# Cross attention: the first scores of a batch in eight steps of two heads, the chain of their maxima one step later

## The chip, the cores and the metric
The kernel runs on one core of a Trainium2 chip. Times are microseconds on the device for one execution, from three runs; the profile is of one further execution. TensorE does matmuls, VectorE and ScalarE read its results from PSUM banks, GpSimd does elementwise work in SBUF, and DMA queues (issued by SyncE, and here also by ScalarE) move data.

## The reference, cut to what matters
Two transformer layers over 8 batches of 112 tokens with 256 features and 16 heads of 16. The part that matters is multi-head attention, which stands three times: cross attention of 112 queries to 375 keys (first layer), self attention (second layer), cross attention to the same 375 tokens with other weights (second layer), then an MLP.

```python
def mha(q, k, v):
    scores = jnp.einsum('bqhd,bkhd->bhqk', q, k) / jnp.sqrt(d)
    attn = jax.nn.softmax(scores, axis=-1)
    out = jnp.einsum('bhqk,bkhd->bqhd', attn, v)
    return out.reshape(B, Nq, C)
x = x + mha(...) @ cross_o_w + cross_o_b
```

The softmax subtracts the largest score of each query and head. The kernel therefore makes the scores twice: once with queries on the partitions, for the maxima ("first scores"), and once transposed, keys on the partitions, with the negative maximum added inside the matmul ("transposed scores"), which go through the exponential and straight into the product with the values.

## The kernel before, in words
`attend` builds both cross attentions and the self attention. Work goes in slots, one per batch. In slot b the engines finish batch b, make the first scores and maxima of batch b+1 (`LAG` is 1 in cross attention), do the output projection of batch b-1 (the tail), and prepare keys, values and normalised context of later batches (the fills). Slot -1 is a preparing slot: it has first scores and fills, but no transposed scores and no tail. Slots -1 to 6 have first scores; slot 6 has no key fills, slot 7 has no first scores any more.

A cross attention slot has steps u = 0 to 12. Each engine has its own list of instructions in a fixed order, written out by `pe_slot`, `act_slot`, `dve_slot` and `pool_slot`, and the engines meet at semaphores. What TensorE does in a step, in this order:
- four transposed scores of unit u (L651 to L661), two banks in turn, each waiting for the exponential two units back;
- a tail part in steps 1, 3 and 5 (`TAIL_AT`, L679);
- a fill (`FILL_AT`, L607): K0 in step 1, K1 in 3 (keys), V0 in 7, V1 in 9 (values), T0 in 10, T1 in 12 (transposition of the context);
- the first scores of heads `S_AT[u]` to `S_AT[u+1]` (`pe_scores`, L627): one matmul of 375 columns per head, into three banks in turn, so that a head waits until VectorE has reduced the head three before it (`max_done`, L636);
- in step `MAX_AT` the transposition of the maxima (`pe_max_t`, L644), which waits for VectorE's chain (`nm_step`, L645);
- four matmuls with the values (L663 to L677) for the unit of the step before.

VectorE in the same step order: tail work, then for each head of the step a maximum over its 375 scores (L798). After the last head, in step `MAX_AT`, comes the chain of the maxima: four small steps that split the maxima into three bf16 parts (L803, L805, L807, L809), the wait for TensorE's transposition, and the copy of its result (L812); behind that the normalisation of a later context (L766, L769). ScalarE in step `LOAD_MAX_AT` issues the DMA that writes the three parts beside the queries (`load_max`, L848); the first transposed scores of the next slot wait for it (L654). GpSimd splits the keys further (L831, L833) and adds the bias to the new values (L839) after ScalarE has copied a V fill out of PSUM.

Before the change the heads stood 3, 3, 2, 3, 3, 2 in steps 0 to 5, and the chain in step 7:

```python
S_AT = [0, 3, 6, 8, 11, 14, 16, 16, ...] if cross else [0, 2, 4, 4, 4, 4]
LOAD_MAX_AT = 8
MAX_AT = 7 if cross else 3
```

Of the kernel before, what the change touches and what calls it, by code (L numbers as in the profile page):

```python
# [535 lines left out]
def attend(nc, sh, ctx, sems, name, cross, ln, wkv, bk, bv_row, wo, bo_row, gate, stacks, first, ahead=None):  # L536
# [12 lines left out]
    LAG = 1 if cross else 2  # L549


    S_AT = [0, 3, 6, 8, 11, 14, 16, 16, 16, 16, 16, 16, 16, 16] if cross else [0, 2, 4, 4, 4, 4]
    K0, K1, V0, V1, T0, T1 = range(6)
    FILL_AT = {1: K0, 3: K1, 7: V0, 9: V1, 10: T0, 12: T1} if cross else {}
    MID_AT = {4: 0, 6: 1}
    LOAD_MAX_AT = 8
    MAX_AT = 7 if cross else 3
    TAIL_AT = {1: 0, 3: 1, 5: 2} if cross else {1: 0, 2: 1, 4: 2}

    def sb(n, shape, dt=F32):  # L560
# [66 lines left out]
    def pe_scores(pe, b, par, lo, hi, cnt):  # L627
        for i in range(lo, hi):
            if i == 0 and isinstance(b, int) and b == 0:

                pe.wait_ge(stacks.more["stacked"][0], stacks.more["stacked_count"])
            if cross and i == 0:
                pe.wait_ge(stacked[par][0], cnt * 16 * NTERM)
            if cross and i * HS == HC:
                pe.wait_ge(stacked[par][1], cnt * 16 * NTERM)
            wait(pe, max_done, NS * b + (i - 2 if i else 0))  # L636
            for h in range(i * HS, (i + 1) * HS):
                o = (h - i * HS) * T
                w = L if cross else T
                keys_h = sh.k_st[par][0:DEEP, h, 0:w] if cross else sh.k_all[0:DEEP, h, bass.ds(b * T, T)]  # L640
                last = pe.matmul(score[i % 3][:, o:o + w], sh.q_all[0:DEEP, h, bass.ds(b * T, P)], keys_h, start=True, stop=True)  # L641
            last.then_inc(s_psum, 1)

    def pe_max_t(pe, b):  # L644
        pe.wait_ge(nm_step, 4 * b + 4)  # L645

        wait(pe, nm_done, b)
        pe.transpose(nm_bank, nparts[:, :, :].rearrange("t a h -> t (a h)"),
                     sh.ident_bf[0:T, 0:T]).then_inc(nm_psum, 1)
# [49 lines left out]
    def pe_slot(pe, b, par, cnt, has_e, has_s, has_tail):  # L699
        for u in range(NU + 1):  # L700
# [6 lines left out]
            if has_s:  # L707
                pe_scores(pe, b + LAG, (par + LAG) % 2, S_AT[u], S_AT[u + 1], cnt[1])
                if u == MAX_AT:
                    pe_max_t(pe, b + LAG)  # L710
# [3 lines left out]
    def act_slot(act, b, par, cnt, has_e, has_s, has_tail):  # L714
        for u in range(NU + 1):
            if has_e and u < NU:
# [3 lines left out]
                act.activation(prob[u % 2][0:rows, :], score_t[u % 2][0:rows, 0:GH * T], ACT.Exp).then_inc(exp_done, 1)  # L720
            if has_s and cross and u == LOAD_MAX_AT:
                load_max(act, b + LAG, (par + LAG) % 2)
# [36 lines left out]
    def dve_norm_context(dve, b):  # L759

        if not isinstance(b, int) or b > 0:
            dve.wait_ge(fill_psum, fill_no(b - 4, T1) + 1)
        for t in range(NT):
            x_in = sh.ctx[:, bass.ds(b, 1), t, :]
            if ln:
                dve.tensor_scalar(xn[:, t, :], x_in, sh.ctx_mean[:, bass.ds(b, 1), t], sh.ctx_rstd[:, bass.ds(b, 1), t],  # L766
                                  ALU.subtract, ALU.mult).then_inc(xn_done, 1)
            else:
                dve.tensor_copy(xn[:, t, :], x_in).then_inc(xn_done, 1)  # L769

    def dve_slot(dve, b, par, cnt, has_s, has_tail, norm_next):
        for u in range(NU + 1):
# [18 lines left out]
            if has_s:  # L791
                n = b + LAG
                for i in range(S_AT[u], S_AT[u + 1]):
                    dve.wait_ge(s_psum, NS * n + i + 1)
                    if i == 0:
# [3 lines left out]
                                      AX_X, ALU.max, negate=True).then_inc(max_done, 1)  # L799
            if has_s and u == MAX_AT:  # L800
                dve.wait_ge(max_done, NS * (n + 1))
# [10 lines left out]
                dve.tensor_copy(nm_t[(par + LAG) % 2][:, :], nm_bank[0:3 * H, :]).then_inc(nm_done, 1)  # L812
            if norm_next and u == MAX_AT:
                dve_norm_context(dve, b + 3)
# [33 lines left out]
    def load_max(eng, b, par):  # L848

        eng.wait_ge(nm_done, b + 1)  # L850
        eng.dma_start(sh.q_all[DEEP:AUG, :, bass.ds(b * T, T)], nm_t[par][:, :]).then_inc(nm_in[par], 16)
# [280 lines left out]
def first_layer(nc, sh, ins):  # L1132

    with ExitStack() as ctx:
# [6 lines left out]
                     tensor_first=[(sh.wq_in, 16 * 8)], mod_first=[(sh.mod_done, NM)], bank_first=[(sh.mod_done, NM)])  # L1141
        w_all = 16 * 13
        at = attend(nc, sh, ctx, sems, "a0", True, True, sh.wkv0, sh.bcol[:, 1, :], 0, sh.wo0, 1, None, pj, {
            "tensor": pj.more["banks_read"] + md.more["banks_read"] + [(sh.consts_done, 4)],
            "gpsimd": pj.more["x_read"], "sync": []}, {
# [54 lines left out]
def self_attention(nc, sh):  # L1200

    with ExitStack() as ctx:
# [4 lines left out]
                     {n: stack for n in ("full", "rest", "part")})  # L1207
        pad_set = sems.new("pad_set")
        at = attend(nc, sh, ctx, sems, "a1", False, False, None, None, 2, sh.wo1, 3, 0, pj, {
            "tensor": pj.more["banks_read"], "gpsimd": pj.more["x_read"] + [(gate_in, 32)],  # L1210
            "sync": pj.more["banks_read"] + [(pad_set, 3)]})
# [39 lines left out]
def cross_attention(nc, sh, ins):  # L1251

    with ExitStack() as ctx:
        sems = ctx.enter_context(Semaphores(nc))
        mlp_in = sems.new("mlp_in")
        pj = project(nc, sh, ctx, sems, "p2", 1e-6, lambda c, b: sh.bcol[:, 4, c:c + 1], lambda c, b: sh.bcol[:, 5, c:c + 1],
                     sh.wq2, sh.bcol[:, 6, :], False, {"xn": Room(sh.v_space), "xt": Room(sh.gate_space[0])})
        at = attend(nc, sh, ctx, sems, "a2", True, False, sh.wkv2, sh.bcol[:, 7, :], 4, sh.wo2, 5, None, pj, {
            "tensor": pj.more["banks_read"], "gpsimd": pj.more["x_read"], "sync": []}, {"tensor": [], "scalar": [], "vector": []})
        block = ctx.enter_context(nc.Block())  # L1260
# [73 lines left out]
```

## Time and profile before

| | |
|---|---|
| time, median of 3 runs | 636.75 us (636.18 to 638.23) |
| profiled execution | 636.35 us, span 634.6 us |
| granted TensorE clock, mean | 0.865 of full speed |
| PE busy | 489.4 us (77% of the span) |
| DVE busy | 336.0 us (53%) |
| ACT busy | 251.8 us (40%) |
| POOL busy | 167.2 us (26%) |
| key transfers (93.8 KB each) | 2.2 us from issue to landing, median |

PE is TensorE's matmuls, PEld its weight loads (one load per matmul, which can run under the matmul before), DVE VectorE, ACT ScalarE, POOL GpSimd, SP SyncE; a "q" behind a name is that engine's queue. A row of a timeline gives start, duration, engine, line and operation, then output and inputs, the count of merged instructions, and in brackets the idle time of the engine before it and what ended that time. A matmul's end is modelled, so that rows of PE can overlap by a little; from the start of one group to the start of the next is what is read here. The shares are means over parts with different limits: the cross attentions' slots run from about 72 to 230 us and from about 411 to 565 us, the self attention lies between them, loading before and the MLP after.

### The profile page before, as it was taken

To read this page: it belongs to the slowest core of one execution; us is meant where nothing else is said; L and a number is where in the kernel's file an instruction comes from. 1 tells how busy PE (TensorE), PEld (TensorE's weight loads), DVE (VectorE), ACT (ScalarE), POOL (GpSimd) and SP (SyncE) were. 2 spreads that over 40 slices of the span, in tenths; PEclk is the share of its full clock that TensorE was granted. 3 is DMA by queue.
4 is the path that set the end of the run, shared out by engine and by line. 5 is a ranking of instruction groups with operands and counts; after the bars stand their busy time and mean duration, and the time that the engine had idled before them with its cause. 6 is when DMAs were issued, how large, how long until landed. Compare 5 with 4: busy or idle time off the path is not lost. (4 is left out here: it accounts for less than half of the span.)

```text
span 634.6 us, 12540 instructions
## 1 busy us (share of the span) xinstructions
PE 489.4 (77%) x4242; PEld 306.0 (48%) x4242; DVE 336.0 (53%) x835; ACT 251.8 (40%) x523; POOL 167.2 (26%) x182
## 2 busy tenths in 40 slices
PE   3846579999999951942399756089999999968997
PEld 3542245555565530621266424045555555537896
DVE  6594255675565429763257364464755564423441
ACT  1202136656665530210134413036566666452221
POOL 7121033422233109810000028033332333100000
PEclk9956579999999975875579957599999999997999
DMA  8996722121222003187400032662221222000000
GB/s 187 226 307 159 132 74 67 48 74 44 67 75 70 7 29 89 43 187 205 104 19 26 9 133 73 175 152 54 69 62 50 73 73 56 21 2 1 15 23 22
DMA packets 66884, 52.38 MB, mean 83 GB/s; under 512 B 11327, under 2 KB 65039, under 8 KB 66839
## 3 DMA queue, kind: packets, MB, share of 16 engines
q1 hardware_dynamic: 66023, 51.61, 32.3%
q8 instruction: 27, 0.44, 0.3%
q10 hardware_dynamic: 816, 0.17, 0.1%
q14 instruction: 18, 0.15, 0.1%
HBM read 25.66 MB, written 6.44 MB: 51 GB/s over the span
## 5 line engine op out<-in xcount | busy, mean ns | idle before, releaser
L798 DVE TENSOR_REDUCE a_nmax<-bank 112x1 f32<-112x375 f32 (+1 forms) x288 | 140.3, 549 | 128.7 <-PE bank L641 128.4
L720 ACT ACTIVATE a_prob<-bank 128x448 f32<-128x448 f32 (+2 forms) x224 | 120.7, 544 | 114.3 <-PE bank L659 110.5
L641 PE MATMUL bank<-k_stack,q_stack_all 96*128 96x375 bf16 x256 | 69.5, 340 | 30.8 <-DMA q_stack_all<-q_parts 16.5
L675 PE MATMUL bank<-a_prob,v_tokens 128*17 128x112 f32 (+2 forms) x1792 | 88.1, 269 | 1.6 <-ACT a_prob L720 1.4
L659 PE MATMUL bank<-q_stack_all,k_stack 99*128 99x112 bf16 (+1 forms) x768 | 72.2, 216 | 0.7 <-issue 0.7
L659 PEld LDWEIGHTS bank<-q_stack_all,k_stack 99*128 99x128 bf16 x768 | 43.3, 98 | 35.0 <-issue 29.1
L612 PE MATMUL bank<-k_stack_all,wkv 128*128 128x375 f32 x128 | 55.3, 560 | 3.6 <-ACT a_kp L732 2.3
L641 PEld LDWEIGHTS bank<-k_stack,q_stack_all 96*128 96x128 bf16 (+1 forms) x256 | 24.9, 100 | 66.9 <-issue 43.4
L675 PEld LDWEIGHTS bank<-a_prob,v_tokens 128*17 128x17 f32 (+2 forms) x1792 | 29.9, 96 | 46.0 <-issue 30.1
L617 PE MATMUL bank<-wkv,k_stack_all 128*128 128x256 f32 (+1 forms) x192 | 48.4, 388 | 0.0
L839 POOL TENSOR_TENSOR v_tokens<-v_tokens,bias_rows 128x256 f32<-128x256 f32 (+1 forms) x48 | 33.2, 706 | 50.0 <-ACT v_tokens L743 50.0
L730 ACT ACTIVATE k_stack_all<-bank,bias_columns 128x375 f32<-128x375 f32 x32 | 18.4, 574 | 63.3 <-PE bank L612 63.3
L617 PEld LDWEIGHTS bank<-wkv,k_stack_all 128*128 128x128 f32 (+1 forms) x192 | 33.6, 188 | 3.6
L612 PEld LDWEIGHTS bank<-k_stack_all,wkv 128*128 128x128 f32 x128 | 25.6, 220 | 16.9 <-ACT a_kp L732 4.5
L624 PE MATMUL bank<-ident,a_xn 128*128 128x128 f32 (+1 forms) x96 | 19.7, 320 | 16.1 <-DVE a_xn L769 4.1
L831 POOL TENSOR_TENSOR k_stack_all<-k_stack_all,v_all 128x375 f32<-128x375 f32 x16 | 14.3, 896 | 65.3 <-ACT v_all L732 65.3
L1108 ACT ACTIVATE mlp_hid<-bank,bias_hidden 128x224 f32<-128x224 f32 x32 | 14.3, 448 | 38.5 <-PE bank L1057 38.5
L696 PE MATMUL bank<-wo,a_ot 128*112 128x256 f32 x96 | 28.1, 418 | 1.3 <-ACT a_ot L725 1.3
L1067 PE MATMUL bank<-k_stack_all,mlp_hid 128*112 128x256 f32 x128 | 28.3, 379 | 0.0
L1057 PE MATMUL bank<-mlp_xt,k_stack_all 128*128 128x224 f32 x128 | 27.0, 372 | 1.4 <-DVE mlp_xt L1027 1.4
L1057 PEld LDWEIGHTS bank<-mlp_xt,k_stack_all 128*128 128x128 f32 x128 | 25.8, 203 | 2.3 <-DVE mlp_xt L1027 1.7
L930 POOL MEMSET k_stack<- 99x144 bf16 x4 | 0.8, 234 | 96.4 <-POOLq L94 96.4
(138 smaller groups left out, 690.1 us busy)
## 6 DMA issues: line engine op xcount, KB each, us to landing
k_stack<-a_kp SPq DMA_DIRECT2D x96, 93.8 KB, 2.2
k_stack<-v_all SPq DMA_DIRECT2D x96, 93.8 KB, 2.2
q_stack_all<-q_parts SPq DMA_DIRECT2D x36, 224.0 KB, 4.4
q_parts<-p_q_part SPq DMA_DIRECT2D x4, 672.0 KB, 4.9
k_stack_all<-k_parts SPq DMA_DIRECT2D x12, 224.0 KB, 4.5
ctx_tokens<-in_ctx_dram SPq DMA_DIRECT2D x2, 1024.0 KB
k_stack_all<-in_L_xcond_mlp_w_dram SPq DMA_DIRECT2D x2, 1024.0 KB
gate<-gate_rows SPq DMA_DIRECT2D x2, 896.0 KB
```

Of the source, the lines that this page charges most:

```text
L612: last = pe.matmul(cx[:, 0:L], wkv[:, c, m * P:(m + 1) * P], ct[par][:, c, :], start=c == 0, stop=c == CH - 1)
L617: last = pe.matmul(cx[0:rows, (t % 2) * C:(t % 2 + 1) * C], ct[1 - par][:, c, t * P:t * P + rows], wkv[:, c, C:2 * C], start=c == 0, stop= ...
L624: last = pe.transpose(cx[:, t * P:t * P + rows], xn[0:rows, t, c * P:(c + 1) * P], sh.ident[0:rows, 0:rows])
L641: last = pe.matmul(score[i % 3][:, o:o + w], sh.q_all[0:DEEP, h, bass.ds(b * T, P)], keys_h, start=True, stop=True)
L659: last = pe.matmul(score_t[u % 2][:, j * T:(j + 1) * T], keys_h, sh.q_all[0:AUG, h, bass.ds(b * T, T)], start=True, stop=True)
L675: last = pe.matmul(pv[32 * j:32 * j + D + 1, g * T:(g + 1) * T], sh.v_sb[par][0:rows, t, h, :], prob[u % 2][0:rows, j * T:(j + 1) * T], st ...
L696: last = pe.matmul(tb[0:T, 0:C], ot[:, c, :], wo[:, c, :], start=c == 0, stop=c == CH - 1)
L720: act.activation(prob[u % 2][0:rows, :], score_t[u % 2][0:rows, 0:GH * T], ACT.Exp).then_inc(exp_done, 1)
L798: dve.tensor_reduce(nmax[:, i * HS:(i + 1) * HS], score[i % 3][0:T, 0:HS * w].rearrange("t (h k) -> t h k", k=w), AX_X, ALU.max, negate=Tr ...
L839: pool.tensor_tensor(v, v, sh.brow[0:keys[t], bv_row, :].rearrange("p (h d) -> p h d", d=D), ALU.add).then_inc(v_done, 1)
L1057: last = pe.matmul(sh.bank[1 + m % 4][:, 0:N2], w1[:, c, m * P:(m + 1) * P], xt[:, c, :], start=c == 0, stop=c == CH - 1)
L1067: last = pe.matmul(y_bank[j][0:T, 0:C], hid[:, m, j * T:(j + 1) * T], w2[:, m, :], start=m == 0, stop=m == NH - 1)
```

## The change
Three constants of `attend` change, for cross attention. The sixteen first scores of a batch stand two in each of steps 0 to 7, the chain of the maxima with TensorE's transposition stands in step 8, and the DMA issue on ScalarE in step 9. Self attention keeps its lists (`LOAD_MAX_AT` is used in cross attention alone). Matmuls, reduces, transfers and buffers stay the same in number and shape; what changes is where they stand in the lists of TensorE, VectorE and ScalarE.

```diff
-    S_AT = [0, 3, 6, 8, 11, 14, 16, 16, 16, 16, 16, 16, 16, 16] if cross else [0, 2, 4, 4, 4, 4]
+    S_AT = [0, 2, 4, 6, 8, 10, 12, 14, 16, 16, 16, 16, 16, 16] if cross else [0, 2, 4, 4, 4, 4]
     K0, K1, V0, V1, T0, T1 = range(6)
     FILL_AT = {1: K0, 3: K1, 7: V0, 9: V1, 10: T0, 12: T1} if cross else {}
     MID_AT = {4: 0, 6: 1}
-    LOAD_MAX_AT = 8
-    MAX_AT = 7 if cross else 3
+    LOAD_MAX_AT = 9
+    MAX_AT = 8 if cross else 3
```

## Rows read from the trace of the kernel before

**Rows 1.** Busy time by stretch, one slot: us, busy (count) per engine, clock, DMA, GB/s
```profile
108.08:127.25 19.17, 18.77 (x201) 10.90 (x197) 11.27 (x27) 11.90 (x26) 6.35 (x8) 1.00 0.25 62
```
**Rows 2.** Timeline of the same slot, TensorE's matmuls: start, duration, engine, line, operation
```profile
112.40 0.74 PE L641 MATMUL bank<-k_stack,q_stack_all 96*128 96x375 bf16 x2
...
113.07 0.39 PE L675 MATMUL bank<-a_prob,v_tokens 128*17 128x112 f32 x8
...
115.08 0.64 PE L641 MATMUL bank<-k_stack,q_stack_all 96*128 96x375 bf16 x3
...
116.18 1.19 PE L641 MATMUL bank<-k_stack,q_stack_all 96*128 96x375 bf16 x3
...
117.30 0.39 PE L675 MATMUL bank<-a_prob,v_tokens 128*17 128x112 f32 x8
...
118.74 0.48 PE L641 MATMUL bank<-k_stack,q_stack_all 96*128 96x375 bf16 x2
...
119.15 0.39 PE L675 MATMUL bank<-a_prob,v_tokens 128*17 128x112 f32 x8
...
119.47 0.37 PE L659 MATMUL bank<-q_stack_all,k_stack 99*128 x4
...
119.77 0.39 PE L675 MATMUL bank<-a_prob,v_tokens 119*17 119x112 f32 x8
...
120.30 1.95 PE L617 MATMUL bank<-wkv,k_stack_all 128*128 128x256 f32 x8
...
122.09 0.21 PE L648 MATMUL bank<-ident_bf,a_nparts 112*128 112x112 bf16 x1
...
122.23 0.39 PE L675 MATMUL bank<-a_prob,v_tokens 128*17 128x112 f32 x8
```
**Rows 3.** Timeline of the same slot, VectorE: reduces, output addition, first and last chain step
```profile
115.44 2.82 DVE L798 TENSOR_REDUCE a_nmax<-bank 112x1 f32<-112x375 f32 x6 [1.41 <-PE bank L641]
...
119.06 0.42 DVE L785 TENSOR_TENSOR x_tokens<-bank,x_tokens 112x256 f32 x1 [0.79 <-PE bank L696]
...
119.40 0.99 DVE L798 TENSOR_REDUCE a_nmax<-bank 112x1 f32<-112x375 f32 x2
...
120.43 0.17 DVE L803 CAST a_nparts<-a_nmax 112x16 bf16<-112x16 f32 x1
...
121.05 0.17 DVE L809 TENSOR_TENSOR a_nparts<-a_nrest,a_nparts 112x16 bf16<-112x16 f32 x1
```
**Rows 4.** Timeline of the preparing slot of the first layer, VectorE and TensorE
```profile
78.90 3.73 DVE L798 TENSOR_REDUCE a_nmax<-bank 112x1 f32<-112x375 f32 x8 [0.67 <-PE bank L641]
...
82.88 0.82 DVE L805 TENSOR_TENSOR a_nrest<-a_nmax,a_nparts 112x16 f32<-112x16 f32 x1
...
83.94 0.17 DVE L809 TENSOR_TENSOR a_nparts<-a_nrest,a_nparts 112x16 bf16<-112x16 f32 x1
...
84.16 0.10 PEld L648 LDWEIGHTS bank<-ident_bf,a_nparts 112*128 112x128 bf16 x1 [1.18 <-DVE a_nparts L809]
...
84.23 1.08 PE L617 MATMUL bank<-wkv,k_stack_all 128*119 128x256 f32 x4
```
**Rows 5.** Timelines of two slots, GpSimd's additions and a chain step beside one
```profile
123.02 1.44 POOL L839 TENSOR_TENSOR v_tokens<-v_tokens,bias_rows 128x256 f32<-128x256 f32 x2 [0.80 <-ACT v_tokens L743]
...
139.82 0.90 POOL L833 TENSOR_TENSOR a_kp<-k_stack_all,a_kp 128x375 bf16<-128x375 f32 x1 [1.75 <-ACT a_kp L736]
139.91 0.85 DVE L809 TENSOR_TENSOR a_nparts<-a_nrest,a_nparts 112x16 bf16<-112x16 f32 x1
```
**Rows 6.** Timeline of the first slot, the issue of the maxima's DMA
```profile
123.08 0.79 ACTq L851 DMA_DIRECT2D q_stack_all<-a_nm_t  x1
```
**Rows 7.** Waits of weight loads in slot 6, first layer, then second: us, times, longest
```profile
PEld bank L641 <- DVE a_nmax L798: 2.1, 7, 0.4
...
PEld bank L641 <- DMA k_stack<-v_all: 1.0, 1, 1.0
```
**Rows 8.** Waits of weight loads over six slots, 88 to 205 us: us, times, longest
```profile
PEld bank L624 <- ACT k_stack_all L750: 2.1, 6, 1.0
```

## The prediction, made before the changed kernel ran

> **What bounds the kernel now.** I read the page first, then the busy time by stretch, then the timeline of one slot engine by engine, and last who waited for whom. The change touches only the slots of the two cross attention layers, so everything is read from one such slot, the one from 108.08 to 127.25 us. There TensorE has work for 18.77 of 19.17 us at a granted clock of 1.00, which is the 2.4 GHz level; VectorE has 11.27, ScalarE 11.90, GpSimd 6.35 [rows 1]. TensorE carries out its list in order, so a slot lasts as long as its matmuls plus the stops inside that list. The matmuls stay the same; the forecast is the difference of the stops.
>
> I write S14 for the score matmul of head 14, h14 for its reduce on VectorE, and "values", "transposed scores" for the two groups of four in each step. A score of head i goes to bank i mod 3 and so waits until the reduce of head i-3 is done.
>
> **Stops that the change removes.** The two scores of step 2 begin at 112.40 and the values behind them at 113.07: 0.67 us. An undisturbed pair takes 0.41 (118.74 to 119.15), so 0.26 is a stop. The three of step 4 take 1.12 (116.18 to 117.30); undisturbed they would take 0.41 plus 0.16 for a third head (375 columns at the 2.4 GHz level), so 0.55 is a stop [rows 2]. VectorE shows the cause: six reduces without a gap from 115.44, 0.47 each, which TensorE has to follow [rows 3]. Together 0.81 us per slot. With two heads per step these stops go: S5, S7, S9 and S11 each need the reduce of three heads before, which lies at least one whole step back and, but for S9 and S13, has a fill or a tail behind it; for S9 I count the reduce done just in time.
>
> **A stop that stays in another place.** S13 needs h10. VectorE works on the output addition of the tail at 119.06 and takes the next reduce at 119.40 [rows 3]; in the new order that reduce is h10, done at 119.87. In step 4 of before the values start 0.45 after the end of the reduce that the last score waits for (115.44 + 3 x 0.47 = 116.85, values 117.30), so the values of step 6 start at 120.32. Without a stop they would start at 119.77 + 2 x 0.16 = 120.09 [rows 2]. Cost 0.23 (bounds 0 and 0.26, the stop of the pair above).
>
> **The stop that the change adds.** Today S14 and S15 stand in step 5 and the transposition of the maxima in step 7 behind the V0 fill; TensorE reaches it at 122.09, long after VectorE's chain of four small steps (120.43 to 121.05 + 0.17 = 121.22) [rows 2, 3]. In the new order S14 and S15 stand behind the V0 fill in step 7, and between them and the transposition in step 8 lie only one group of values and one of transposed scores. Call Y the start of the first matmul behind the V0 fill (122.09 in this slot).
> - TensorE's side: pair of scores 0.41, values 0.32 (119.15 to 119.47), transposed scores 0.30 (119.47 to 119.77), transposition 0.14 (122.09 to 122.23) [rows 2]. Without a wait the next work starts at Y + 1.17.
> - VectorE's side: a reduce starts 0.36 after its score (115.08 to 115.44), two reduces and the gap to the chain take 1.03 (119.40 to 120.43), the chain 0.79 [rows 2, 3]. The chain ends at Y + 2.18. In the slot that only prepares (below) TensorE does wait here today: chain ends at 83.94 + 0.17, weight load at 84.16 after 1.18 us of waiting, next matmul at 84.23 [rows 4]. So 0.12 more: Y + 2.30.
>
> The stop is 1.13 us if nothing disturbs the chain. Queued behind the waiting transposition are all of TensorE's work of steps 8 to 12 and the next slot; nothing of it can pass.
>
> **What disturbs the chain.** GpSimd adds the bias to the values of the V0 fill, two additions that start 0.93 after the point that I call Y and last 1.44 (123.02 to 124.46); today that is after the chain. In the new order the chain's second step comes at Y + 1.6 and lies inside them. In this trace a chain step that meets a GpSimd addition waits to its end: GpSimd 139.82 to 140.72, the chain's fourth step from 139.91 to 140.76 instead of 0.17 us [rows 5]; in the preparing slot the second step took 0.82 in the same way [rows 4]. By this the second step ends near Y + 2.3 to Y + 2.4 instead of Y + 1.77 and the chain 0.5 to 0.6 later; I take 0.55. Its bounds are 0 (the steps slip between the additions) and 0.68 (the longer of the two holds, 0.85 for 0.17). The stop is then 1.68.
>
> The Trainium skill, page "SBUF — State Buffer", section "SBUF: two separate sides", says that a VectorE operation with two SBUF inputs and a GpSimd operation that reads SBUF take a shared port pair as an exclusive lock, and that the later one blocks fully. The holds just told agree; no row of before shows these two bias additions against a chain step. By the rule the stop is 1.68, by a chain that runs free it is 1.13.
>
> **The rest of the step that moves.** The copy of the transposed maxima and the DMA that spreads them (one issue on ScalarE's queue) move with the transposition. The issue is at 123.08, 4.2 us ahead of the next slot [rows 1, 6]. From the transposition to the slot's end remain all steps but one (0.62), and the issue stands behind the exponential of step 9 instead of step 8: I count 3 us or more from issue to need, against 2.2 for the larger key transfers on the page's list. Cost 0; if that cover were gone, the excess would stop the first transposed scores. VectorE's context normalisation also follows the chain and must be done by the T0 fill of step 10, one step (0.62) fewer away than now, but clear of GpSimd's two additions: cost 0, bound 0.3. SP's queue has nothing that moves, and its key transfers gain time.
>
> **The sum.** Each layer has eight slots with first scores.
> - Slots 0 to 5: 1.68 + 0.23 - 0.81 = +1.10 each; 12 of them, +13.2 us.
> - Slot 6 has no key fills, so today its scores stop more often: 7 waits with 2.1 us in the first layer, of which some 0.16 each is the ordinary loading gap, so 1.0 real; about 0.9 goes (bounds 0 and 2.1). In the second layer it also waits 1.0 us for keys by DMA [rows 7]; the eighth score comes a step later and the slot before grows behind that issue, so 0.9 more goes. 1.68 - 0.9 and 1.68 - 1.8: +0.7 together.
> - The preparing slot (-1), where VectorE sets the pace: today eight reduces run without a gap from 78.90 while the V0 fill runs under the last ones [rows 4]. In the new order S14 waits for that fill: from the end of h10 it is 0.45 until the fill starts (as to the values in step 4), 1.79 for it (120.30 to 122.09) [rows 2], 0.36 and 0.95 for the two reduces, 3.55 against 5 x 0.47 = 2.35 now; and h10 ends some 0.4 later, since h6 and h7 come behind the K1 fill and not ahead of it (2 x 0.47, less one reduce by which that fill starts earlier). That is +1.6, less 0.65 of a hold that today's chain has there (82.88, 0.82 for 0.17), plus 0.55: +1.5 each, +3.0 (bounds 0.9 and 2.0 each).
>
> Together 13.2 + 0.7 + 3.0 = +16.9 us. The profiled execution took 636.35 us (634.6 of span), so 653.3. It lies 0.4 under the median of 636.75, less than the sum can tell; I say 653.
>
> **Rivals.**
> 1. The chain runs free of GpSimd: 12 x (1.13 + 0.23 - 0.81) + (2 x 1.13 - 2.7) + 2 x 0.95 = 8.1, so 644.4 us. For it: the hold depends on which engine starts first, and the casts of the chain were never seen held. Against: two additions without a gap cover 1.4 us, just where the chain's two-input steps fall.
> 2. Faster. The stop before the transposition is made up in steps 9 to 12, if these wait for ScalarE and not for TensorE: then only the removed stops count, 12 x 0.58 + 2.7 gained, 3.0 lost in the preparing slots, near 629.7. It decides from about 1.2 us recovered per slot. For it: ScalarE has over half of the slot in work [rows 1]. Against: over six slots TensorE's loads waited 2.1 us for ScalarE's copies of the context, six times, the largest such sum there, 0.35 per slot [rows 8], and what ScalarE works on in these steps is made by TensorE behind the stop, so it cannot run ahead.
> 3. The removed stops do not come back as time, because the exponentials or key copies of steps 2 to 5 take over the pace: +12 x 0.81 and +2.7 on top, 666 us. Against: each stop that I count follows a reduce [rows 3], and TensorE has hardly a gap beside them [rows 1].
>
> **Chances.** Forecast (held chain) 0.60, rival 1 0.22, rival 2 0.06, something between (most of the stop made up, within 0.3%) 0.05, rival 3 0.07. A measurement of this kernel tells 0.3% (1.9 us) from no change. Faster 0.06, same 0.05, slower 0.89. The range goes from 642 (rival 1 with S13 at nothing, 644.4 - 12 x 0.23) to 658 (the forecast with the longer hold in all 16 slots, and nothing saved in slot 6); about 2 in 10 lie outside.
>
> **What would show it.** In the new trace: TensorE's weight load of the maxima's transposition waiting 1 to 2 us for the chain's last step in every slot; scores in pairs with no stop but one in step 6; two-input chain steps of 0.5 to 0.8 us beside GpSimd's bias additions; slots 1 us longer at an unchanged clock. It is wrong if the transposition does not wait, or if the slots do not grow by what it waits less 0.6.

## The result, and the profile after

The changed kernel takes 665.9 us (median of four runs, 662.3 to 669.3) against 637.5 for the kernel before (636.2 to 642.9, four runs): ratio 1.043 with a 95% interval of 1.034 to 1.052. It is slower, as forecast, but by 28.4 us and not by 16.9, and it lies 8 us above the top of the range, 658. The profiled execution took 668.65 us.

The page of the changed kernel (busy us, share of the span, instructions by engine):

```profile
span 666.9 us, 12540 instructions
...
PE 497.2 (75%) x4242; PEld 311.3 (47%) x4242; DVE 336.6 (50%) x835; ACT 251.1 (38%) x523; POOL 166.2 (25%) x182
```

The span grew by 32.3 us with the same number of instructions. TensorE's busy time grew by 7.8 (489.4 before), although its list has the same matmuls: some ran slower. The rest, 24.5, is time in which it stood.

Busy time by stretch: the slot that answers to [rows 1], then every stretch inside the slots in which the granted clock stood at 0.50, the 1.2 GHz level:

```profile
111.70:132.30 20.60, 18.68 (x201) 10.87 (x198) 11.19 (x27) 11.87 (x26) 6.24 (x8) 1.00 0.23 58
...
170.80:174.20 3.40, 3.40 (x37) 1.59 (x35) 0.19 (x1) 1.97 (x4) 1.36 (x2) 0.50 0.01 3
...
191.30:194.60 3.30, 3.30 (x22) 2.08 (x21) 1.05 (x3) 1.03 (x3) 0.64 (x1) 0.50 0.02 6
...
440.40:447.20 6.80, 5.75 (x22) 3.47 (x21) 1.46 (x5) 2.33 (x5) 1.37 (x2) 0.50 0.31 82
...
481.50:484.80 3.30, 3.30 (x37) 1.84 (x30) 0.00 (x0) 1.93 (x4) 1.37 (x2) 0.50 0.01 3
...
501.90:505.30 3.40, 3.40 (x30) 1.69 (x28) 0.00 (x0) 1.62 (x4) 1.37 (x2) 0.50 0.03 8
...
563.40:566.60 3.20, 3.20 (x27) 1.78 (x25) 0.00 (x0) 1.00 (x3) 0.60 (x1) 0.50 0.02 3
```

The first line is the forecast slot: 1.43 us longer at the 2.4 GHz level, with TensorE's work the same to 0.1 us. The other six are what the forecast did not have; the long one, from 440.40, follows the preparing slot of the second layer. Behind the preparing slot of the first layer the clock is low for 6.8 us in both kernels; elsewhere in its slots the kernel before has no such stretch.

The timeline of that slot, TensorE and its weight loads, VectorE, GpSimd and the DMA issue (answers to [rows 2, 3, 5, 6]):

```profile
121.22 0.42 DVE L785 TENSOR_TENSOR x_tokens<-bank,x_tokens 112x256 f32 x1 [0.80 <-PE bank L696]
121.56 1.90 DVE L798 TENSOR_REDUCE a_nmax<-bank 112x1 f32<-112x375 f32 x4
...
121.84 0.73 PE L641 MATMUL bank<-k_stack,q_stack_all 96*128 96x375 bf16 x2
...
122.51 0.39 PE L675 MATMUL bank<-a_prob,v_tokens 119*17 119x112 f32 x8
...
123.03 1.95 PE L617 MATMUL bank<-wkv,k_stack_all 128*128 128x256 f32 x8
...
124.82 0.48 PE L641 MATMUL bank<-k_stack,q_stack_all 96*128 96x375 bf16 x2
...
125.19 1.00 DVE L798 TENSOR_REDUCE a_nmax<-bank 112x1 f32<-112x375 f32 x2 [1.72 <-PE bank L641]
...
125.76 1.31 POOL L839 TENSOR_TENSOR v_tokens<-v_tokens,bias_rows 128x256 f32<-128x256 f32 x2 [1.38 <-ACT v_tokens L743]
...
126.22 0.24 DVE L803 CAST a_nparts<-a_nmax 112x16 bf16<-112x16 f32 x1
...
126.50 0.60 DVE L805 TENSOR_TENSOR a_nrest<-a_nmax,a_nparts 112x16 f32<-112x16 f32 x1
...
127.35 0.17 DVE L809 TENSOR_TENSOR a_nparts<-a_nrest,a_nparts 112x16 bf16<-112x16 f32 x1
...
127.58 0.10 PEld L648 LDWEIGHTS bank<-ident_bf,a_nparts 112*128 112x128 bf16 x1 [1.81 <-DVE a_nparts L809]
...
127.73 0.39 PE L675 MATMUL bank<-a_prob,v_tokens 128*17 128x112 f32 x8
128.58 0.79 ACTq L851 DMA_DIRECT2D q_stack_all<-a_nm_t  x1
```

Read it from the bottom up. The transposition's weight load has waited 1.81 us for the last step of the chain; the chain's second step (L805) took 0.60 instead of 0.17 and ended with GpSimd's additions (125.76 + 1.31 = 127.07; 126.50 + 0.60 = 127.10). The first values behind it start at Y + 2.91, with Y = 124.82.

The same wait in the preparing slot (answers to [rows 4]; timeline of the first layer):

```profile
85.99 0.60 DVE L805 TENSOR_TENSOR a_nrest<-a_nmax,a_nparts 112x16 f32<-112x16 f32 x1
...
87.06 0.10 PEld L648 LDWEIGHTS bank<-ident_bf,a_nparts 112*128 112x128 bf16 x1 [2.65 <-DVE a_nparts L809]
```

And over the whole run (waits of weight loads: us, times, longest):

```profile
PEld bank L648 <- DVE a_nparts L809: 37.8, 22, 2.7
```

Of the 22, 16 are in the cross attention slots: 14 of 1.81 and two of 2.65 us. The other six stand in self attention, as before.

### The profile page after: what moved, and what is told of

It reads as the page before. It is cut to its first block and busy times, and to the rows that moved or that the text cites. A ratio compares the mean times of both kernels' runs of the same rounds, so it can differ in the third digit from the quotient of the medians.

```text
span 666.9 us, 12540 instructions
## 1 busy us (share of the span) xinstructions
PE 497.2 (75%) x4242; PEld 311.3 (47%) x4242; DVE 336.6 (50%) x835; ACT 251.1 (38%) x523; POOL 166.2 (25%) x182
## 5 line engine op out<-in xcount | busy, mean ns | idle before, releaser
L798 DVE TENSOR_REDUCE a_nmax<-bank 112x1 f32<-112x375 f32 (+1 forms) x288 | 142.7, 550 | 166.4 <-PE bank L641 166.2
L675 PE MATMUL bank<-a_prob,v_tokens 128*17 128x112 f32 (+2 forms) x1792 | 90.2, 275 | 1.6 <-ACT a_prob L720 1.5
L641 PE MATMUL bank<-k_stack,q_stack_all 96*128 96x375 bf16 x256 | 67.2, 334 | 28.1 <-DMA q_stack_all<-q_parts 16.7
L659 PE MATMUL bank<-q_stack_all,k_stack 99*128 99x112 bf16 (+1 forms) x768 | 74.3, 221 | 0.7 <-issue 0.7
L659 PEld LDWEIGHTS bank<-q_stack_all,k_stack 99*128 99x128 bf16 x768 | 44.7, 100 | 36.5 <-issue 31.1
L617 PE MATMUL bank<-wkv,k_stack_all 128*128 128x256 f32 (+1 forms) x192 | 51.5, 406 | 0.0
L624 PE MATMUL bank<-ident,a_xn 128*128 128x128 f32 (+1 forms) x96 | 22.0, 351 | 16.1 <-DVE a_xn L769 4.1
L648 PE MATMUL bank<-ident_bf,a_nparts 112*128 112x112 bf16 x24 | 5.6, 234 | 33.7 <-DVE a_nparts L809 33.7
L696 PE MATMUL bank<-wo,a_ot 128*112 128x256 f32 x96 | 29.7, 436 | 1.3 <-ACT a_ot L725 1.3
L743 ACT ACTIVATE v_tokens<-bank 128x256 f32<-128x256 f32 (+1 forms) x48 | 16.7, 382 | 34.1 <-PE bank L617 33.3
```

The source lines that it names most:

```text
L617: last = pe.matmul(cx[0:rows, (t % 2) * C:(t % 2 + 1) * C], ct[1 - par][:, c, t * P:t * P + rows], wkv[:, c, C:2 * C], start=c == 0, stop= ...
L624: last = pe.transpose(cx[:, t * P:t * P + rows], xn[0:rows, t, c * P:(c + 1) * P], sh.ident[0:rows, 0:rows])
L659: last = pe.matmul(score_t[u % 2][:, j * T:(j + 1) * T], keys_h, sh.q_all[0:AUG, h, bass.ds(b * T, T)], start=True, stop=True)
L675: last = pe.matmul(pv[32 * j:32 * j + D + 1, g * T:(g + 1) * T], sh.v_sb[par][0:rows, t, h, :], prob[u % 2][0:rows, j * T:(j + 1) * T], st ...
L696: last = pe.matmul(tb[0:T, 0:C], ot[:, c, :], wo[:, c, :], start=c == 0, stop=c == CH - 1)
L798: dve.tensor_reduce(nmax[:, i * HS:(i + 1) * HS], score[i % 3][0:T, 0:HS * w].rearrange("t (h k) -> t h k", k=w), AX_X, ALU.max, negate=Tr ...
```

## The experiments

Theory A, the forecast's: the kernel is slower because the last pair of scores stands behind the V0 fill with too little before the transposition, part of it through GpSimd's hold. Theory E came with the result: what the sum lacks is the lower granted clock behind some of the stops. Each ratio is to the kernel before, run beside it: 638.5 us with the first four experiments, 639.9 with the others. "V0 to M" below is the time from the start of the V0 fill to the transposition: 1.79 before, 4.55 after.

**The last pair ahead of the V0 fill**, all else as changed:

```
-if u in FILL_AT and has_fill(b, FILL_AT[u]):
+if u != 7 and u in FILL_AT and has_fill(b, FILL_AT[u]):
     pe_fill(...)
 ... scores of step u ...
+if u == 7 and u in FILL_AT and has_fill(b, FILL_AT[u]):
+    pe_fill(...)
```

> Undoes one part: in step 7 the last two first scores stand ahead of the V0 fill instead of behind it; eight steps of two heads and the chain in step 8 stay. Theory A (the stop before the maxima's transposition, caused by the last two scores behind the fill, makes the change slow, and draws the granted clock down): TensorE does not wait for the chain any more except in the preparing slots, no stretch at half clock between 96 and 230 us or between the second layer's first slot and its last, the stops of steps 2 and 4 stay away; 12 x 0.58 + 2.7 less than before, so 627 to 630 us. Rival B (two heads per step is itself the slower order, since other work sets the pace of steps 2 to 5): 640 us or more, with new gaps in steps 0 to 6.

Measured: 630.1 us, ratio 0.987 (0.984 to 0.991), at the upper end of the expectation. Timeline of one slot (line numbers are three higher than in the changed kernel), then the busy time over five slots of the first layer:

```profile
118.27 0.48 PE L641 MATMUL bank<-k_stack,q_stack_all 96*128 96x375 bf16 x2
...
118.59 1.90 PE L617 MATMUL bank<-wkv,k_stack_all 128*128 128x256 f32 x8
...
120.29 0.18 DVE L812 TENSOR_TENSOR a_nparts<-a_nrest,a_nparts 112x16 bf16<-112x16 f32 x1
...
120.95 0.21 PE L648 MATMUL bank<-ident_bf,a_nparts 112*128 112x112 bf16 x1
```
```profile
96.00:211.00 115.00, 112.71 (x1252) 65.98 (x1254) 70.76 (x173) 72.31 (x152) 36.87 (x47) 1.00 0.25 62
```

The chain is done (120.29 + 0.18) half a microsecond before TensorE comes to it, so the stop is gone, and the clock stays up. (In the preparing slots a wait of 0.54 is left, and one low stretch follows the first of them, as in the kernel before.) Swapping one pair with one fill is worth 36 us and turns the change into a gain. This is the fastest version found: two heads in each step do save time, provided that the last two stand ahead of the fill.

**The chain alone one step later**, heads as before:

```
-S_AT = [0, 2, 4, 6, 8, 10, 12, 14, 16, ...]
+S_AT = [0, 3, 6, 8, 11, 14, 16, 16, 16, ...]
```

> One part alone: heads 3, 3, 2, 3, 3, 2 in steps 0 to 5 as before, but the chain in step 8 and the DMA issue in step 9. Theory A: the transposition finds the chain done, the stops of steps 2 and 4 are as before; 635 to 639 us, the same. Rival C (the later chain is the cost, by the normalisation or the maxima's DMA being late at step 10 or at the next slot): 3 us slower or more, with TensorE waiting at the T0 fill or at the first transposed scores.

Measured: 639.65 us, ratio 1.000 (0.998 to 1.003). The later transposition, its DMA and the context normalisation behind it cost nothing that the time can tell, as the forecast had it. The trace shows a small cost all the same. Timeline of one slot, ScalarE's DMA issue and its copy of the V1 values, then the weight load of the T0 fill, here and in the kernel before:

```profile
125.05 1.08 PE L617 MATMUL bank<-wkv,k_stack_all 128*119 128x256 f32 x4
...
125.36 0.79 ACTq L851 DMA_DIRECT2D q_stack_all<-a_nm_t  x1
...
126.33 0.39 ACT L743 ACTIVATE v_tokens<-bank 119x256 f32<-119x256 f32 x1 [0.55 <-PE bank L617]
...
126.85 0.31 PEld L624 LDWEIGHTS bank<-ident,a_xn 128*128 128x128 f32 x3 [0.26 <-DVE a_xn L766]
```
```profile
123.38 1.08 PE L617 MATMUL bank<-wkv,k_stack_all 128*119 128x256 f32 x4
...
124.50 0.39 ACT L743 ACTIVATE v_tokens<-bank 119x256 f32<-119x256 f32 x1
...
125.01 0.31 PEld L624 LDWEIGHTS bank<-ident,a_xn 128*128 128x128 f32 x3
```

The copy starts 0.20 behind the end of the V1 fill instead of 0.04, and the T0 fill, which follows the copy by 0.12 to 0.13 both times, comes later with it: from the transposed scores of step 10 to the T0 fill the ten full slots take 4.59 us together instead of 2.93, 0.17 more each. The profile puts the wait down to the normalisation, but that ended at 126.54, 0.18 ahead of the copy. The DMA issue now stands directly ahead of the copy in ScalarE's list, and ends at 126.15; that it is what holds the copy is argued from the list, since no run moves the issue alone.

**GpSimd's first bias addition behind the chain**, all else as changed:

```
+if t == 0:
+    pool.wait_ge(nm_step, 4 * (b + LAG) + 4)
```

> The changed kernel, with GpSimd's bias additions on the new values held until the chain of the maxima is done (one more wait on GpSimd); takes away the hold of the chain. Theory A with the hold: the chain's second step falls from 0.60 to 0.17 us, TensorE's wait from 1.81 to some 1.2 to 1.3 us, 16 x 0.55 = 9 us less and fewer stretches at half clock: 648 to 657 us. Rival D (the chain is slow for another reason, or GpSimd's additions are needed earlier): the wait stays at 1.8, or the time stays at 662 to 669.

Measured: 649.6 us, ratio 1.019 (1.014 to 1.023). Timeline of one slot (GpSimd's line numbers are two higher), then the slots of the first layer by stretch:

```profile
123.73 0.17 DVE L805 TENSOR_TENSOR a_nrest<-a_nmax,a_nparts 112x16 f32<-112x16 f32 x1
...
124.37 0.10 PEld L648 LDWEIGHTS bank<-ident_bf,a_nparts 112*128 112x128 bf16 x1 [1.31 <-DVE a_nparts L809]
...
124.40 1.33 POOL L841 TENSOR_TENSOR v_tokens<-v_tokens,bias_rows 128x256 f32<-128x256 f32 x2 [3.07 <-DVE a_nparts L809]
```
```profile
96.00:230.00 134.00, 123.30 (x1376) 71.65 (x1378) 71.53 (x176) 78.97 (x166) 39.29 (x51) 1.00 0.21 53
```

With the additions out of the way the second chain step takes its 0.17 and the wait is 1.31 instead of 1.81: the hold is real and worth 0.5 us per slot, 8 us in 16. But 16 us have come back between the medians, and the clock is 1.00 in the whole stretch. So the hold also costs indirectly: at 1.81 the clock falls behind some stops, at 1.31 in this profile behind none of the 14.

**TensorE kept at work during the stop**: 14 matmuls of 224 columns, whose results nobody reads, just ahead of the wait (and a wait for the bank that they write):

```
+wait(pe, tb_free, b)
+for _ in range(14):
+    pe.matmul(tb[:, 288:512], sh.ident_bf[0:DEEP, :], sh.q_all[0:DEEP, 0, 0:224], start=True, stop=True)
 wait for the chain; transposition
```

> The changed kernel with 14 matmuls of 224 columns (bf16, results never read) put on TensorE ahead of the transposition's wait, some 1.3 us of work inside the stop of 1.8. They add nothing to the computation. Theory E (the stop draws the granted clock to its lower level for stretches of 3.4 us and more, and this is what my forecast lacked): the slots are as long as the changed kernel's undisturbed ones, no half clock from the second slot on, 652 to 657 us and runs close to each other. Rival F (the half-clock stretches have another cause, or the stop is not TensorE's): 662 to 669 as the changed kernel, or more by the work added (up to 20 us).

Measured: 659.7 us (657.2 to 660.2, four runs), ratio 1.032 (1.028 to 1.037), somewhat over the expectation. Timeline of one slot (line numbers four higher), then the slots of the first layer by stretch:

```profile
124.24 1.51 PE L648 MATMUL bank<-q_stack_all,ident_bf 96*128 96x224 bf16 x14
...
126.07 0.22 PE L652 MATMUL bank<-ident_bf,a_nparts 112*128 112x112 bf16 x1 [0.32 <-DVE a_nparts L813]
```
```profile
96.00:226.00 130.00, 125.00 (x1352) 75.92 (x1350) 72.55 (x175) 73.56 (x154) 38.27 (x50) 1.00 0.22 55
```

The transposition comes no earlier (V0 to M is 4.55 as in the changed kernel), so the chain's delay is all there. The weight load still waits, but 0.57 us, and behind none of the 14 stops does the clock fall; the only stretch at half clock is one of 3.4 us behind the first preparing slot. The profiled span is 657.7 against 666.9. The 9.2 us between the two profiles are what idling adds to the delay, as far as one pair of profiles can tell; the medians are 6.2 apart, and the changed kernel's profile is one of its slower runs. The stretches at half clock explain most of the 9.2: a short one costs some 1.1 (the pitch from one transposition to the next is 21.46 instead of 20.40, 21.43 instead of 20.24, 21.27 instead of 20.23, 22.08 instead of 20.87) and the long one 2.4 (19.31 instead of 16.92); the fifth short one stands in a pitch that grew by 2.0 (18.91 instead of 16.92). Together that is 8.9; the rest is the sum of differences of both signs outside the full slots.

With hardly any low clock in its slots this kernel is still 21.3 us over the kernel before run beside it, where the forecast had 16.9. So the clock is not all that the forecast lacked.

**The chain in step 7 again**, that is directly behind the pair of scores, so that the stop is longer:

```
-LOAD_MAX_AT = 9
-MAX_AT = 8 if cross else 3
+LOAD_MAX_AT = 8
+MAX_AT = 7 if cross else 3
```

> The changed kernel with the chain and TensorE's transposition one step earlier, in step 7 right behind the last two scores (the DMA issue in step 8): one group of values and one of transposed scores fewer cover the stop. Theory A with E: the wait grows by 0.62 from 1.81 to some 2.4 us, so 16 x 0.62 = 10 us more, and more stretches at half clock than the changed kernel's five in the slots: 672 to 690 us. Rival F (the half-clock stretches have nothing to do with the stop): the wait grows, the stretches stay about five or fewer, 672 to 678 us. Rival G (the wait before the transposition is made up elsewhere): 662 to 669 us.

Measured: 682.6 us, ratio 1.068 (1.064 to 1.072). A slot's wait, then a stretch at half clock and the slots of the second layer:

```profile
129.13 0.10 PEld L648 LDWEIGHTS bank<-ident_bf,a_nparts 112*128 112x128 bf16 x1 [2.65 <-DVE a_nparts L809]
```
```profile
108.70:112.10 3.40, 3.40 (x32) 1.55 (x30) 0.00 (x0) 2.04 (x4) 1.37 (x2) 0.50 0.03 8
...
454.00:595.00 141.00, 124.12 (x1278) 71.75 (x1277) 72.26 (x178) 73.38 (x156) 38.74 (x50) 0.93 0.20 51
```

V0 to M is again 4.55: the chain comes as late behind the fill as it did. But one group of values and one of transposed scores, 0.62 us, no longer cover the stop and stand behind the transposition; the weight load's wait grew by 0.84. The kernel lost another 15 us against the changed kernel run beside it (667.6, below). By the pitches of slots without a low clock (20.94, 20.26 instead of 20.32, 19.79 in the kernel that was kept at work) some 0.4 to 0.6 of each slot's growth is that uncovered work. The rest goes with the clock: ten stretches at half clock begin at or behind the end of one of the 16 stops of 2.65, nine without the one behind the first preparing slot, three of these long; the mean clock of the second layer's slots fell to 0.93. Over all runs the mean granted clock is 0.834 to 0.846 here, 0.848 to 0.860 in the eight runs of the changed kernel, and 0.864 to 0.877 in those of the two kernels with stops of 1.31 and 0.57. Longer standing, lower clock.

**The changed kernel once more**, no edit:

> The changed kernel again, on this chip, for the spread of its runs. Theory E (stretches at half clock behind the stops): times between 657 and 670 us that fall as the mean granted clock of the run rises, a profile with between 0 and 7 such stretches in the slots, and the time less some 1.5 us per stretch near 658. Rival F: time and clock do not go together.

Measured: 667.6 us (662.1 to 669.2), ratio 1.041 (1.036 to 1.046). The four runs, by time: 662.1 at a mean granted clock of 0.860, 666.4 at 0.850, 668.9 at 0.853, 669.2 at 0.849; the first four were 662.3 and 663.2 at 0.860, 668.7 at 0.848, 669.3 at 0.849. Two of the stretches in its profile:

```profile
458.70:465.40 6.70, 6.70 (x62) 4.16 (x62) 1.00 (x2) 4.07 (x8) 1.37 (x2) 0.50 0.27 66
...
561.10:564.40 3.30, 3.30 (x24) 1.91 (x27) 0.00 (x0) 0.95 (x3) 0.56 (x1) 0.50 0.01 3
```

Four stretches stand in the slots of this profile, one short and three long, in part behind other stops than the first profile's. So which stops are followed by a lower clock changes from run to run. The time follows the clock over 7 us, with one pair of runs the other way round (0.850 and 0.853). The expected 1.5 us per stretch does not fit: it would put this profile, 669.2 with four stretches, at 663 without them and not at 658. The kernel that was kept at work (657.2 to 660.2) lies below all eight.

**The pair ahead of the fill by another route**: heads spread less evenly, the chain where it was before the change:

```
+S_AT = [0, 3, 5, 7, 9, 12, 14, 16, ...]
+LOAD_MAX_AT = 8
+MAX_AT = 7 if cross else 3
```

> Heads 3, 2, 2, 2, 3, 2, 2 in steps 0 to 6, chain in step 7 and DMA issue in step 8 as before the change: pairs mostly, and all scores ahead of the V0 fill, which covers the chain. Theory A: no wait before the transposition but in the preparing slots, about one short score stop left in steps 4 and 6 each, no half clock in the slots after the first: 627 to 633 us. Rival B (pairs are the slower order): 640 us or more.

Measured: 633.6 us (630.9 to 639.9), ratio 0.989 (0.985 to 0.993), a little over the expectation but the same in kind: all heads before the fill, and a gain. TensorE still waits for the chain, 0.2 to 0.5 us in most slots. Its slowest run is the profiled one, and that has a stretch at half clock in the second layer, in the last slot that has first scores. Weight load ahead of it, and the stretch by the busy time:

```profile
542.40 0.10 PEld L641 LDWEIGHTS bank<-k_stack,q_stack_all 96*128 96x128 bf16 x1 [1.57 <-DMA k_stack<-v_all]
```
```profile
542.60:549.40 6.80, 6.80 (x48) 3.30 (x47) 3.34 (x7) 1.33 (x3) 0.00 (x0) 0.50 0.00 0
```

This stop is a wait for keys and has nothing to do with the chain. The kernel with the chain alone late has the same: 1.48 us of waiting for keys, then 6.8 us at half clock. So in these two places a low clock followed a stop that had another cause.

**The stop at S13.** In the fastest version VectorE takes the output addition of step 5 behind that step's reduces instead of ahead of them:

```
 step u on VectorE:
+    reduces of step u
     if TAIL_AT.get(u) == 2: output addition
-    reduces of step u
```

> As e1 (scores of step 7 ahead of the V0 fill), and VectorE takes the tail's output addition of step 5 behind that step's two reduces instead of ahead of them, so that h10 is done earlier. Theory A: the stop at S13 in step 6 goes (0.23 to 0.26 in 12 slots): 3 us less than e1, so 625 to 629 us. Rival H (that stop is covered by something else, an exponential or a copy): the time of e1, 628 to 632 us.

Measured: 633.0 us (630.0 to 633.6), ratio 0.990 (0.987 to 0.992): no gain over the 630.1 of the version it was built on. A miss, and the timeline shows why:

```profile
115.94 0.48 PE L641 MATMUL bank<-k_stack,q_stack_all 96*128 96x375 bf16 x2
...
116.28 0.41 DVE L797 TENSOR_TENSOR x_tokens<-bank,x_tokens 112x256 f32 x1
...
116.88 0.74 PE L641 MATMUL bank<-k_stack,q_stack_all 96*128 96x375 bf16 x2
```

The pair S12, S13 (115.94) runs without a stop now, and the next pair has it instead: S15 needs h12, which by the order of the list stands behind the addition. The addition costs VectorE 0.4 us wherever it goes, and one of the scores close behind pays.

## Why the prediction was right in kind and short in size

Held, step by step:

- The removed stops. From the slot's start to its V0 fill went 12.21 us before (108.09 to 120.30) and 11.31 after (111.72 to 123.03); 0.32 of that is the two heads that went behind the fill, so 0.58 was saved, as forecast (0.81 less 0.23). The stop at S13 is there: the values stand 0.67 behind the start of the pair (121.84 to 122.51), 0.26 more than undisturbed; 0.23 was forecast.
- The added stop. The chain begins at Y + 1.40 (forecast 1.39) and the next values at Y + 2.91 (forecast 2.85), so the stop is 1.74 against 1.68. The hold by GpSimd is there, so rival 1 is out; the experiment with the additions behind the chain took it away. By the lock that the Trainium skill describes (page "SBUF — State Buffer", section "SBUF: two separate sides") the second step had to wait to the end of the additions: it did (0.60 us, to 127.10), and with them gone took 0.17. The first cast, with one input, took 0.24 beside them and ended at 126.46, where the first of the two additions ended (125.76 and half of 1.31 make 126.42); so it may have been held as well.
- The DMA and the other work that moves. Cost 0 was forecast (bound 0.3 for the normalisation). The experiment with the chain alone late shows no difference in time, but 0.17 us per full slot at the T0 fill.
- Rival 2 (629.7 us) is out for this kernel, since nothing of the stop was made up. The rival's number is nearly that of the version without the stop (630.1). Rival 3 is out too, although its 666 is nearest to the result: it had the removed stops not coming back, and they did, by 0.58 in the slot shown.

Failed: **"slots 1 us longer at an unchanged clock"**. The sum had a term for the time that TensorE stands, and none for the matmuls behind it that run at the 1.2 GHz level; and its term for the full slot was too small. By the profiles the 32.3 us are:

| | forecast | measured |
|---|---|---|
| ten pitches between full slots | +11.0 | +14.7 |
| pitches at the edges, slot 6 | +2.9 | +4.0 |
| preparing slots, all outside the slots | +3.0 | +4.4 |
| matmuls at the lower clock | 0 | +9.2 |
| sum | +16.9 | +32.3 |

The first three measured values are of the kernel that was kept at work, which has the same chain and no lower clock behind its 14 stops; the last is the changed kernel less that one. The nine microseconds at the bottom are the largest of the errors, and they were not among the rivals either. They are one pair of profiles; by the medians the last line is 6.2 (665.9 less 659.7).

The second error is the full slot, +1.47 in the mean instead of +1.10. Three small terms make up 0.32 of the 0.37. The saving is smaller: the version without the stop is only 0.39 per slot faster than the kernel before, in the mean over these slots, and not 0.58. Its T0 fill comes 0.17 later per slot (4.60 us in ten slots instead of 2.93), as in the experiment with the chain alone late; in the slot shown of the changed kernel the same was 0.12. The last pair takes 0.41 behind the fill, and 0.32 ahead of it (118.27 to 118.59 in the version without the stop); the sum took its place as free, which is 0.09. And the stop is 1.74 instead of 1.68. In the preparing slot the term was right: its transposition is 2.90 later (87.06 against 84.16), 1.6 of it because its first load came later in that profile, so +1.3 against +1.5.

Open: why the clock falls behind some stops of 1.81 us and not behind others of the same length.

## What to carry to other kernels

When a change puts a wait into the list of an engine that works in order, count what stands between the last producer's input and the wait; here one pair of scores on the wrong side of one fill decided between -1.3% and +4.3%. Look as well at what a moved DMA issue stands ahead of in the list of the engine that issues it: here it was the copy that the next fill waits for, by argument from the list, at 0.17 us a slot. When the engine that waits is TensorE, add a term for the matmuls behind each stop: look in the trace at the granted clock behind the stops that are already there, and give it a rival of its own where none is as long as the new one. To tell the two apart, keep the engine at work through the wait and see what comes back.

## What the runs showed of the hardware that was not expected

In the changed kernel's first profile five of the 14 stops of 1.81 us were followed by 3.4 us at the 1.2 GHz level, and the stop of 2.65 us in the second layer's preparing slot by 6.8 us, each beginning 0.5 to 2.0 us behind the end of the stop. In its second profile it was three of the 14, one for 3.4 and two for 6.8 us. Behind the 14 stops of 1.31 there was none, behind the 16 of 2.65 there were ten. Two stops of 1.48 and 1.57 us, in other kernels and for another reason (keys), were followed by 6.8 us. A stretch of 3.4 us cost 1.0 to 1.2 us in four pitches and 2.0 in a fifth, one of 6.8 us 2.4. The places differ between profiles of the same kernel, and its runs spread over 7 us, where the kernel that works through the stops spreads over 3.
